# Four layer norms that centre all their blocks first, the first layer's second norm directly behind its first, and the gate's softmax laid between later steps

## What is computed

```
xn = layernorm(x)                 # no gain, no bias
s  = attn_l(xn);  g = silu(ffn_l(xn))
x  = x + s * g
```

```
# attn_0
gated = clip(layernorm(xn)*g1+b1 @ qW1 + b, -1, 1)     # qW = W + (sign(W) - W)
x1    = xn + gated @ qW2 + b2
qx    = clip(x1 * 128 / (max|x1| of the group + eps))  # 4 groups along the sequence
out   = qx + mamba(layernorm(qx)*g2+b2)                # in_proj, conv, scan, out_proj
# ffn_0
probs = softmax over the sequence of (xn @ gate_w + gate_b)    # 8 experts
top 2 of each row, three products per expert, a weighted sum per expert, mixed back
# ffn_1
probs = softmax(xn @ router_w), top 2, shares; w13, silu(gate)*up, w2, weighted
```

## Time and profile before

| | |
|---|---|
| median of 3 executions | 1225.59 us (1221.81 to 1227.93) |
| the profiled execution | 1225.27 us, its span 1223.5 us |
| mean granted TensorE clock | 0.973 |
| busy share of the span: PE, DVE, ACT, POOL | 91%, 74%, 66%, 46% |

### The profile page before, as it was taken

One profiled execution on the slowest core, in us unless ns is written; L12 is line 12 of the kernel. 1 busy time (PEld: TensorE's weight loads), 2 busy tenths in 40 slices (PEclk: granted clock), 3 DMA queues, 4 the chain that ended last, 5 costly groups with the idle time before them and its releaser, 6 DMA issues.

```text
span 1223.5 us, 14560 instructions
## 1 busy us (share of the span) xinstructions
PE 1115.2 (91%) x4908; PEld 604.2 (49%) x4908; DVE 900.4 (74%) x1368; ACT 806.1 (66%) x1187; POOL 564.3 (46%) x310
## 2 busy tenths in 40 slices
PE   5778899999998989999878999999999999989887
PEld 1323344444434445454456666666666666523554
DVE  3567999999994453524578999999999999544454
ACT  4558667676634343512678999999999999556432
POOL 6002799898950964633004554554554454500000
PEclk8889899999998999989998999999999999989999
DMA  3000655555550211110021211111121121000000
GB/s 128 0 1 15 207 190 172 197 173 197 179 210 18 88 47 40 43 35 22 0 57 31 78 46 51 55 54 47 53 60 46 53 61 45 16 1 1 1 1 35
DMA packets 36665, 84.23 MB, mean 69 GB/s; under 512 B 7110, under 2 KB 13031, under 8 KB 36327
## 3 DMA queue, kind: packets, MB, share of 16 engines
q1 hardware_dynamic: 36590, 83.29, 21.7%
HBM read 80.72 MB, written 2.56 MB: 68 GB/s over the span
## 4 chain that ended last, share of the span: by engine, by line
PE 41%; DVE 32%; ACT 12%; issue 8%; POOL 6%; DMA 0%; DVEq 0%; SPq 0%; POOLq 0%; ACTq 0%
DVE work L1632 6%; PE ps L1002 5%; DVE work L668 5%; POOL work L729 4%; PE ps L1018 3%; PE ps L1010 3%; DVE work L1704 3%; DVE work L1716 3%; PE ps L1257 3%; DVE yd L1727 3%; DVE work L1682 2%; DVE work L1730 2%; ACT ps L565 2%; PE ps L449 2%; PE ps L2000 2%
## 5 line engine op out<-in xcount | busy, mean ns | idle before, releaser
L1802 POOL TENSOR_TENSOR ssum<-ssum,rs 128x1024 f32<-128x1024 f32 x32 | 75.8, 2369 | 198.1 <-DVE work L1632 195.8
L668 DVE TENSOR_TENSOR_SCAN work<-ps,work 128x1024 f32<-128x1024 f32 x64 | 146.6, 2291 | 8.2
L1632 DVE SCALAR_TENSOR_TENSOR work<-work,w_t 128x1024 f32<-128x1024 f32 x96 | 123.3, 1284 | 14.6 <-ACT work L1466 11.9
L449 PE MATMUL ps<-work,ident 128*128 128x512 f32 x256 | 121.8, 598 | 5.6 <-POOL work L729 5.4
L992 POOL TENSOR_TENSOR work<-work,ssum 128x1024 f32<-128x1024 f32 x32 | 76.2, 2387 | 109.0 <-DVE work L1081 58.1
L565 ACT ACTIVATE ps<-work,A 128x1024 f32<-128x1024 f32 x64 | 71.6, 1118 | 72.4 <-DVE work L668 72.4
L1081 DVE TENSOR_TENSOR work<-work,ps 128x512 f32<-128x512 f32 x64 | 43.9, 688 | 99.9 <-PE ps L1010 99.9
L1060 ACT ACTIVATE work<-ps 128x512 f32<-128x512 f32 x64 | 38.1, 597 | 115.4 <-PE ps L1002 115.4
L729 POOL TENSOR_TENSOR work<-work 128x1024 f32<-128x1024 f32 x42 | 99.1, 2362 | 13.6 <-DVE work L668 13.6
L1810 POOL TENSOR_TENSOR yd<-yd,work 128x896 f32<-128x896 f32 x32 | 66.9, 2092 | 46.2 <-DVE work L1730 46.0
L1704 DVE SCALAR_TENSOR_TENSOR work<-work,ps 128x64 f32<-128x64 f32 x384 | 79.1, 276 | 4.0 <-DVE work L1704 0.9
(11 more groups left out here) (370 smaller groups left out, 2552.7 us busy)
## 6 DMA issues: line engine op xcount, KB each, us to landing
work<-bc_rows SPq DMA_DIRECT2D x42, 512.0 KB, 3.7
work<-sdo_rows SPq DMA_DIRECT2D x64, 224.0 KB, 3.6
yd<-bc_rows SPq DMA_DIRECT2D x22, 512.0 KB, 3.7
rs<-w_rows SPq DMA_DIRECT2D x32, 256.0 KB, 4.1
ssum<-share_rows SPq DMA_DIRECT2D x32, 256.0 KB, 3.2
w_t<-in_tile_w SPq DMA_DIRECT2D x32, 195.5 KB, 2.6
work<-in_w SPq DMA_DIRECT2D x1, 2048.0 KB, 7.9
shared<-in_f SPq DMA_DIRECT2D x3, 512.0 KB, 5.7
```

Source lines behind the costliest of these rows:

```text
L449: mm = pe.matmul(ps[:, YACC + h, :], ident[:, :], HS[u % 4][:, h * BL:(h + 1) * BL], start=(n == 0), stop=(n == DS - 1))
L668: dve.tensor_tensor_scan(h, flat_pair(DABANK), h, 0.0, ALU.mult, ALU.add).then_inc(m0["scan"], 1)
L1632: c = dve.scalar_tensor_tensor(HC[u], HP[:, tap:tap + SEQ], par(u, "taps", tap), HC[u], ALU.mult, ALU.add)
```

## The change

A second form of the PE part, `wide_norm_pe`, has four banks for the means, so that no mean waits for a centring. DVE's part is split in `centre_dve` and `scale_dve`, and norms 0 to 3 call the four centrings ahead of the first scaling (in norms 2 and 3 with other steps between them). Norm 1 stands directly behind norm 0 on PE, and its centrings ahead of the weights' folding on DVE. The logits move behind norm 1 on PE, in banks 6 and 7: two ahead of the up products, two behind those of block 0. The maxima move behind the clips, the exponentials behind the evictions of the up products, the division and the 16 transposes into norm 2, and the copy of the probabilities behind it. POOL's three selects on `sel` wait for the last block of norm 1. At layer 1, the two open output projections stand behind means 0 and 1, and all the router's logits ahead of the first gate products. No arithmetic is added or removed. The core of the diff:

```diff
+        WIDE = (0, 1, 4, 5)
+        def wide_norm_pe(pe, r, src, ready=None, ready_at=0, between=None, use=None):
+            def mean(k):
...
+                pe.matmul(ps[:, WIDE[k], :], ones_d[:, :], blk(src, k), start=True, stop=True).then_inc(norm["mean"], 1)
...
+            mean(0)
+            mean(1)
+            if between is not None:
+                between()
+            mean(2)
+            var(0)
+            mean(3)
+            var(1)
+            var(2)
+            follow(0)
+            follow(1)
+            var(3)
+            follow(2)
+            follow(3)
         def l0_up_pe(pe):
-            norm_pe(pe, 1, XN, norm["out"])
+            wide_norm_pe(pe, 1, XN, norm["out"])
+            f0_logits_pe(pe, 0)
+            f0_logits_pe(pe, 1)
             pe.wait_ge(m0["dve"], m0["weff"] + 1)
+            pe.wait_ge(norm["centred"], NB * 1 + NB)
             for k in range(NB):
                 pe.wait_ge(norm["out"], NB * 1 + k + 1)
+                if k == 1:
+                    f0_logits_pe(pe, 2)
+                    f0_logits_pe(pe, 3)
+                    pe.wait_ge(f0["act"], f0["lg"] + NB)
...
         def l0_pe(pe):
             pe.wait_ge(load["weights"], 16 * len(FIRST))
-            norm_pe(pe, 2, X1, m0["dve"], m0["scaled"])
+            wide_norm_pe(pe, 2, X1, m0["dve"], m0["scaled"])
+            pe.wait_ge(norm["centred"], NB * 2 + NB)
+            f0_probs_pe(pe)
...
             norm_act(act, 1, H0)
-            for k in range(NB):
+            f0_logits_act(act, 0)
+            f0_logits_act(act, 1)
+            for k in range(NB):
+                if k == 1:
+                    f0_logits_act(act, 2)
+                    f0_logits_act(act, 3)
...
         def l0_norm_dve(dve, own):
+            for k in range(NB):
+                centre_dve(dve, 1, XN, H0, k)
             dve.wait_ge(m0["act"], m0["sign"] + 3)
...
-            norm_dve(dve, own, 1, XN, H0, V("ln1_g"), V("ln1_b"))
+            for k in range(NB):
+                scale_dve(dve, own, 1, H0, k, V("ln1_g"), V("ln1_b"))
         def l0_clip_dve(dve):
...
+            for b in range(BATCH):
+                dve.wait_ge(f0["act"], f0["lg"] + (b + 1) * NB // BATCH)
+                dve.tensor_reduce(gmx[0:E, b:b + 1], lg[:, b * SEQ:(b + 1) * SEQ], AX.X, ALU.max, negate=True).then_inc(f0["dve"], 1)
...
         def l0_dve(dve, own):
+            l0_scale_dve(dve, own, 0)
+            l0_scale_dve(dve, own, 1)
+            centre_dve(dve, 2, X1, H0, 0)
+            l0_scale_dve(dve, own, 2)
+            centre_dve(dve, 2, X1, H0, 1)
+            l0_scale_dve(dve, own, 3)
+            centre_dve(dve, 2, X1, H0, 2)
+            centre_dve(dve, 2, X1, H0, 3)
+            f0_probs_dve(dve, own)
+            for k in range(NB):
+                scale_dve(dve, own, 2, H0, k, V("ln2_g"), V("ln2_b"))
+            f0_probs_out_dve(dve)
             own(dve.memset(pad[:, :, 0:DC - 1], 0.0))
-            norm_dve(dve, own, 2, X1, H0, V("ln2_g"), V("ln2_b"))
...
         def f0_act(act, own):
...
+            l0_up_act(act)
             for b in range(BATCH):
                 act.wait_ge(f0["dve"], f0["top"] + b + 1)
...
-            l0_up_act(act)
...
             def logits(k):
...
                 if k == NB - 1:
                     mm.then_inc(m1["pe"], 1)
-                    ups(0)
-                if k == NB - 2:
                     pe.wait_ge(load["experts"], 16 * len(EXPERTS))
                     gates(0)
+                    ups(0)
...
+            pe.wait_ge(f0["act"], f0["g"] + 2)
+            wide_norm_pe(pe, 3, X, f0["dve"], f0["x_out"], rest, logits)
...
-            norm_dve(dve, own, 3, X, XN, first=lambda k: l0_rest_dve(dve, own, k))
+            l0_last_dve(dve, own)
+            centre_dve(dve, 3, X, XN, 0)
+            centre_dve(dve, 3, X, XN, 1)
+            l0_out_dve(dve, own, 2)
+            l0_out_dve(dve, own, 3)
+            centre_dve(dve, 3, X, XN, 2)
+            scale_dve(dve, own, 3, XN, 0)
+            scale_dve(dve, own, 3, XN, 1)
+            centre_dve(dve, 3, X, XN, 3)
+            scale_dve(dve, own, 3, XN, 2)
+            scale_dve(dve, own, 3, XN, 3)
...
+            pool.wait_ge(norm["out"], 2 * NB)
             for k in range(3):
                 ins = pool.affine_select(sel[:, :, :], sel[:, :, :], [[-1, H2], [0, P]], ALU.not_equal, 1.0,
```

More of the change, by code:

```diff
@@ L260, in norm_pe, with var, follow, centre_dve @@
                     use(k)
+        WIDE = (0, 1, 4, 5)
+        def wide_norm_pe(pe, r, src, ready=None, ready_at=0, between=None, use=None):
+            def mean(k):
+                if ready is not None:
+                    pe.wait_ge(ready, ready_at + k + 1)
+                pe.matmul(ps[:, WIDE[k], :], ones_d[:, :], blk(src, k), start=True, stop=True).then_inc(norm["mean"], 1)
+            def var(k):
+                pe.wait_ge(norm["square"], NB * r + k + 1)
+                if k >= 2:
+                    pe.wait_ge(norm["log"], NB * r + k - 1)
+                pe.matmul(ps[:, 2 + k % 2, :], ones_d[:, :], sq[:, k % 2, :], start=True, stop=True).then_inc(norm["var"], 1)
+            def follow(k):
+                if use is not None:
+                    pe.wait_ge(norm["out"], NB * r + k + 1)
+                    use(k)
+            mean(0)
[12 more added lines that the diff above has]
+            follow(3)
+        def centre_dve(dve, r, src, dst, k):
+            dve.wait_ge(norm["mean"], NB * r + k + 1)
+            dve.tensor_tensor(blk(dst, k), blk(src, k), ps[:, WIDE[k], :], ALU.subtract).then_inc(norm["centred"], 1)
+        def scale_dve(dve, own, r, dst, k, gain=None, bias=None):
+            dve.wait_ge(norm["rstd"], NB * r + k + 1)
+            mul = dve.tensor_tensor(blk(dst, k), blk(dst, k), rs[:, k % 2, :], ALU.mult)
+            if gain is None:
+                mul.then_inc(norm["out"], 1)
+            else:
+                own(mul)
+                dve.tensor_scalar(blk(dst, k), blk(dst, k), gain, bias, ALU.mult, ALU.add).then_inc(norm["out"], 1)
         def norm_dve(dve, own, r, src, dst, gain=None, bias=None, first=None):
@@ L818, in f0_mix_pe, with f0_logits_act @@
             pe.matmul(ps[:, MIX_BANK[k], :], vT[:, :], blk(rtf[0:E, :], k), start=True, stop=True).then_inc(f0["pe"], 1)
+        def f0_logits_act(act, k):
+            act.wait_ge(f0["pe"], f0["logit"] + k + 1)
+            act.activation(blk(lg, k), ps[0:E, 6 + k % 2, :], ACT.Identity, bias=V("gate_b", 0, E)).then_inc(f0["act"], 1)
         def f0_act(act, own):
-            for k in range(NB):
-                act.wait_ge(f0["pe"], f0["logit"] + k + 1)
-                act.activation(blk(lg, k), ps[0:E, 4 + k, :], ACT.Identity, bias=V("gate_b", 0, E)).then_inc(f0["act"], 1)
+            l0_up_act(act)
             for b in range(BATCH):
@@ L834, in f0_dve, with f0_probs_dve @@
         def f0_dve(dve, own):
-            for b in range(BATCH):
-                dve.wait_ge(f0["act"], f0["lg"] + (b + 1) * NB // BATCH)
-                dve.tensor_reduce(gmx[0:E, b:b + 1], lg[:, b * SEQ:(b + 1) * SEQ], AX.X, ALU.max, negate=True).then_inc(f0["dve"], 1)
             l0_norm_dve(dve, own)
+            l0_clip_dve(dve)
+            l0_peak_dve(dve, own)
+            l0_factor_dve(dve, own)
+        def f0_probs_dve(dve, own):
             dve.wait_ge(f0["act"], f0["exps"] + BATCH)
@@ L843, in f0_dve, with f0_probs_out_dve @@
                                   ALU.mult).then_inc(f0["dve"], 1)
-            l0_clip_dve(dve)
-            l0_peak_dve(dve, own)
+        def f0_probs_out_dve(dve):
             dve.wait_ge(f0["pe"], f0["probs_T"] + 1)
             dve.wait_ge(const["ready"], 2)
-            dve.tensor_copy(rw[:, 0], ps[:, 2, 0:NT * E].rearrange("p (i e) -> p i e", e=E)).then_inc(f0["dve"], 1)
-            l0_factor_dve(dve, own)
-            for k in range(NB):
-                l0_scale_dve(dve, own, k)
+            dve.tensor_copy(rw[:, 0], ps[:, PROBS_BANK, 0:NT * E].rearrange("p (i e) -> p i e", e=E)).then_inc(f0["dve"], 1)
         def f0_route_dve(dve, own):
@@ L1026, in logits, with rest @@
                     mm.then_inc(m1["pe"], 1)
[L1027 to L1028 removed]
                     pe.wait_ge(load["experts"], 16 * len(EXPERTS))
                     gates(0)
[L1032 to L1039 removed]
+                    ups(0)
+            def rest():
+                out_project(pe, 2)
+                out_project(pe, 3)
+            pe.wait_ge(f0["act"], f0["g"] + 2)
+            wide_norm_pe(pe, 3, X, f0["dve"], f0["x_out"], rest, logits)
             for n in range(1, N1 + LAG):
@@ L2269, in _ @@
             dve.wait_ge(const["ready"], 1)
-            norm_dve(dve, own, 0, X, XN)
+            for k in range(NB):
+                centre_dve(dve, 0, X, XN, k)
+            for k in range(NB):
+                scale_dve(dve, own, 0, XN, k)
             f0_dve(dve, own)
```

30 lines of the change are left out of this document (10 added, 20 removed).

## The result

The change makes the kernel faster: 1207.4 us (median of 4 runs, 1206.4 to 1208.7) against 1225.5 for the kernel before on the same chip (9 runs, 1221.8 to 1227.6), a ratio of 0.9855 with a 95% interval of 0.9835 to 0.9875. On another chip it had been 1209.0 against 1226.6 (0.9853, 0.982 to 0.9885). The forecast was 1207, range 1197 to 1215.

A forecast was written before the change was run, and what follows sets the result against it. No engine bounds the whole; in the norms DVE and ACT take turns, and the rest of the front is serial. Gains 8.7 (peak) + 4.0 (third norm) + 5.7 (fourth norm) = 18.4 us; 1225.3 - 18.4 = 1206.9, say 1207, range 1197 to 1215.

The forecast's parts named there:

- the front: First 97 us, through the input projection: gains of 8.7 us at the group peak and 4.0 in the third norm.
- the fourth norm: Second layer's start, about 361 to 390 us: new norm and TensorE order gain 5.7 us, bounds 5.0 and 6.5.
- First norm: Kernel start: ACT becomes the bound, last scaling near 19.3 us instead of 24.52, gain 5.2 us.
- Second norm: Directly behind the first: DVE-bound scaling, all out at 30.5, taken as 31.3 us, against 47.81 before.
- Logits and up products: TensorE behind the second norm: last up evicted at 38.9, taken as 39.7 us; downs start there, before 54.58.
- The selects: GpSimd's three selects stand over DVE's clips after the second norm and hold them; gain 8.7 us at the peak.
- the rival without contention: Clips after the second norm aren't held: peak gain 13.5 to 14.9 us, total 1201 us; chance 0.28.
- Third norm: From quantising to the input projection's first eviction, 18.4 us before: gain 4.4, or 2.8 at half clock; 4.0 taken.
- so I carry the gain through: Behind 392 us no instruction's own cost changes, so the summed 18.4 us reaches the end, give or take a few us.
- The slower one: Second layer, 390 to 600 us: TensorE's clock falls and the gain is spent, 1240 us at 0.83; chance 0.03.
- The clock rival: TensorE at half clock in second norm, ups and downs: up to 7.6 us, total 1212 us; chance 0.15.

The follow-up runs named there:

- e2: The changed kernel with the first select at once and the other two waiting for the last clip: 1207.4 us, ratio 0.9855.
- e7: e2 with one more all-reduce, on values nobody reads, behind the first select: 1201.1 us in a single execution.
- e9: The same kernel as e7, timed over five executions: 1202.0 us, ratio 0.981 against the kernel before.
- e8: The changed kernel with the fourth norm and the order of router logits, gates and ups put back as before: 1207.6 us, ratio 0.9862.
- e11: e9 with the second layer's first norm (the fourth norm) put back as before: 1201.6 us, ratio 0.9822.

## Why the prediction was right

The total is: 1207 against 1207.4. Its sum was 18.4 us, the measured one 18.2 at the second layer's start and 17.8 at the end. That it is so near is partly luck: the front brought 13.6 us at the first eviction where 12.7 were added up, and the fourth norm 4.9 where 5.7 were. Term by term, by the prediction's own steps:

*First norm.* Gain 5.2 forecast, 5.7 measured. ACT set the pace, every multiply took 0.69, and TensorE stood at full clock, as said.

*Second norm.* Out at 30.18: the working gave 30.5, and the 0.8 added for a fall of the clock wasn't needed (the windows from 12 to 44 us are all at 1.00). Scaling at 1.18 a block, 1.2 forecast.

*Logits and up products.* The last up was evicted by 39.23, forecast 38.9, or 39.7 with the 0.8.

*The selects.* This was the term on which the forecast turned, and the rival without contention had 0.28. Right in kind and size: a clip between each two selects at starts 4 us apart, the peak at 54.01 against 54.5, a gain of 9.2 against the 8.7 taken. The nearest rows, multiplies beside selects, were the right ones to go by, though a clip has one operand in the buffer and a multiply two. The Trainium skill's rule (SBUF — State Buffer, Who interferes with whom) holds for the clips by the rows of 3.9 us; that a tensor_reduce isn't held, the changed kernel can't show, as its reduces came after the selects, but e2's row of 0.69 beside a select agrees with it. Two details were off and cancelled: a select takes 3.8 us and not 3.6, and the first clip was there at 30.40, not 31.5.

But the price that I put on the rival, "6 us lower", was wrong, and so was a sentence that looked harmless: "GpSimd itself is free at about 43.5, so its all-reduce behind the peak is not late." It was not late in the change, since 12.22 us lay between. It would have been as soon as the clips were freed: e2 had a peak at 47.66 and won nothing. The step looked at when GpSimd's instructions end, and not at what its queue does for the next one. In the kernel before those 6 us lay between 22.7 and 63.5 and no row showed them. With them paid early, freeing the clips is worth what the rival said: 6.3 us at the quantisation in e7, and about 5.4 of the time by the medians of e9 and the change, which come from two chips with intervals that just miss each other.

*Third norm.* Gain 4.4 worked out, 4.0 taken, 4.4 measured (69.37 - 55.36 = 14.0 us against 18.4). Here the softmax in front of the scalings and the half clock both cost what was said.

*Fourth norm.* 5.7 forecast, bounds 5.0 to 6.5; 4.9 measured in the trace, just outside. The working put the last logits at full clock; they ran at half, both groups. The timeline of the changed kernel: sixteen products in 3.58 us, where its first eight take 0.95 (1.9 for sixteen):

```profile
356.81 0.95 PE L1100 MATMUL ps<-w_router,work 128*128 128x8 f32 x8
...
361.41 3.58 PE L1100 MATMUL ps<-w_router,work 128*128 128x8 f32 x16 [0.84 <-DVE work L302]
...
365.03 0.29 DVE L1169 TENSOR_REDUCE rm<-ps 128x16 f32<-128x128 f32 x1 [2.34 <-PE ps L1100]
```

The larger failing is that of the step "so I carry the gain through": the term was worked out against a stretch of the kernel before that itself stood at half clock (378.07, 3.61 us for four products). With the front moved by 13 us the old order ran at full clock in both traces (e8, e11), which is worth 3.3 us to it (why it did isn't settled). So the two gains overlap, and their sum is not what the parts give singly. Front alone 16.6, fourth norm alone 4.9, both 18.1 by the medians. The sum came out right because the front's part was worked out with no share of this, and the fourth norm's with all of it.

*Rivals.* The slower one (second layer at a clock under 0.89) didn't occur: the granted clock of the span went from 0.973 to 0.981. The clock rival came in part, inside what I had taken: the last eight down products took 5.37 us, where twice the 1.98 of each earlier group of four is 3.96 and half of the 7.08 of before is 3.54, so 1.4 to 1.8 us.

## What to carry to other kernels

Before an all-reduce of GpSimd stands on the path for the first time, look at what is ahead of it on that queue: its 6 us begin right behind that instruction. If less than that lies between the two, call it once early on values that nobody reads. Only this one instruction was tried here. When a wait is removed and the time doesn't move, look for the one that had been finished under its cover. And don't add up the gains of two parts, if one is measured against a stretch at half clock: the half clock may be gone once the other part has moved, as it was here.

## What the runs showed of the hardware

- A DVE tensor_scalar of 128x512 f32, buffer to buffer, takes 0.41 us alone and up to 4.05 beside a GpSimd affine_select of 96x4096 bf16: it waits until the select is over. Of several queued selects the next goes ahead of the next clip, so each select costs one clip's turn. Two-operand instructions from the buffer are held the same way, down to a 128x4 one (3.66 for 0.16); reduces and instructions with one operand in PSUM are not (0.69 and 0.75 beside a select).
- Before the first partition_all_reduce of a kernel GpSimd needs 5.63 to 6.21 us in which no instruction and no wait shows. They start with the end of the instruction ahead, not with the call's own wait: in the changed kernel, with 12.22 us between the two, none of it shows. They are paid once.
- The granted clock of the same instructions in the same order can be 0.50 in one kernel and 1.00 in another, 16 us of start apart; the products concerned took 3.4 us more at 0.50.
